# Causal attention inside a two-layer kernel: three single score banks in place of two double ones, and a third bank for the rough maxima

## The reference

```
q = (x @ Wq).reshape(B, T, H, Dh)        # B=2, T=1024, H=16, Dh=16; x is layer-normed
k = (x @ Wk).reshape(B, T, H, Dh)
v = (x @ Wv).reshape(B, T, H, Dh)
scores = jnp.einsum('bthd,bshd->bhts', q, k)
mask = jnp.tril(jnp.ones((T, T), dtype=scores.dtype))
scores = scores * mask                    # masked scores are 0, not minus infinity
attn = jax.nn.softmax(scores / T ** 0.5, axis=-1)
out = jnp.einsum('bhts,bshd->bthd', attn, v).reshape(B, T, H * Dh)
return out @ Wo
```

## Time and profile before

| what | value |
|---|---|
| median of 3 runs | 2155.03 us |
| the profiled execution's own time | 2154.63 us |
| its span | 2152.9 us |
| PE busy | 1960.6 us (91%) |
| DVE busy | 1253.0 us (58%) |
| ACT busy | 822.5 us (38%) |
| POOL busy | 889.0 us (41%) |
| attention: start of its first instruction on DVE, first slot, last values | about 272, 342 and 693 us |
| a middle group's 24 slots (group 4) | 44.0 us |

### The profile page before, as it was taken

The page is one execution under the profiler, slowest core; times in us unless marked ns, Lnnn a source line. Parts: engine busy times, 40 slices in busy tenths (PEclk is TensorE's granted clock), DMA queues, the critical chain, the costliest instruction groups (busy, mean ns, idle before and its releaser), DMA issues. The chain is left out here.

```text
span 2152.9 us, 29698 instructions
## 1 busy us (share of the span) xinstructions
PE 1960.6 (91%) x8876; PEld 1279.2 (59%) x8876; DVE 1253.0 (58%) x2704; ACT 822.5 (38%) x1549; POOL 889.0 (41%) x708
## 2 busy tenths in 40 slices
PE   5899958999999789986779999999889999999987
PEld 5676635555655757655646555555566656565566
DVE  6322264666775722227667777777656777777526
ACT  2122243555655212223324444444514444444413
POOL 0344410343223044432026655666425555665732
PEclk9999967999999589997679999999999999999999
DMA  9111241111110811124232212222032222221001
GB/s 395 52 62 64 57 130 30 31 44 32 44 30 1 353 59 60 66 68 166 45 81 56 55 46 52 55 58 58 19 70 59 55 59 59 58 52 46 24 0 52
DMA packets 64617, 150.91 MB, mean 70 GB/s; under 512 B 14320, under 2 KB 19648, under 8 KB 62208
## 3 DMA queue, kind: packets, MB, share of 16 engines
q1 hardware_dynamic: 54240, 120.44, 19.6%
q0 software_dynamic: 9120, 24.92, 3.7%
q10 hardware_dynamic: 1152, 4.19, 0.5%
HBM read 68.95 MB, written 18.61 MB: 41 GB/s over the span
## 5 line engine op out<-in xcount | busy, mean ns | idle before, releaser
L1858 POOL TENSOR_TENSOR mla_PS<-mla_PS,mla_PT 128x1024 f32<-128x1024 f32 x192 | 457.5, 2383 | 232.6 <-ACT mla_PT L2142 225.3
L2142 ACT ACTIVATE mla_PT<-PS 128x512 f32<-128x512 f32 x512 | 297.2, 600 | 390.9 <-PE PS L1962 322.9
L2275 DVE TENSOR_REDUCE mla_MXP<-PS 128x1 f32<-128x512 f32 x512 | 320.9, 679 | 94.9 <-PE PS L1943 94.4
L1971 PE MATMUL PS<-mla_PT,mla_CN 128*64 128x512 f32 x1024 | 249.4, 607 | 2.3 <-ACT mla_PT L2142 2.3
L1283 DVE TENSOR_REDUCE att_MX<-PS 128x1 f32<-128x512 f32 (+3 forms) x304 | 194.2, 660 | 89.7 <-PE PS L994 49.3
L522 DVE COPY moe_HT<-PS 128x256 f32<-128x256 f32 x188 | 70.4, 415 | 299.9 <-PE PS L648 299.9
L2287 DVE RECIPROCAL PS<-PS 128x128 f32<-128x128 f32 x128 | 114.9, 936 | 180.4 <-PE PS L1978 180.4
L1962 PE MATMUL PS<-mla_QH,mla_KH 113*128 113x512 f32 x512 | 216.1, 422 | 0.9 <-ACT mla_PT L2142 0.9
L684 POOL DMA_INDIRECT moe_XS<-rows_in,moe_GI x96 | 93.7, 976 | 266.1 <-PE PS L634 130.8
L1943 PE MATMUL PS<-mla_KH,mla_QH 113*128 113x512 f32 x512 | 184.8, 429 | 20.6 <-DMA mla_KL<-mla_SL 14.0
L1962 PE MATMUL PS<-mla_QL,mla_KH 113*128 113x512 f32 x512 | 202.4, 395 | 0.0
(11 more groups left out here) (295 smaller groups left out, 3175.8 us busy)
## 6 DMA issues: line engine op xcount, KB each, us to landing
W<-in_W_dram SPq DMA_DIRECT2D x16, 2048.0 KB, 28.1
mla_QH<-mla_SH SPq DMA_DIRECT2D x64, 128.0 KB, 2.4
mla_KH<-mla_SH SPq DMA_DIRECT2D x64, 128.0 KB, 2.4
mla_QL<-mla_SL SPq DMA_DIRECT2D x64, 128.0 KB, 2.4
mla_KL<-mla_SL SPq DMA_DIRECT2D x64, 128.0 KB, 2.4
mla_KH<-mla_SH SPq DMA_DIRECT2D x64, 96.0 KB, 2.3
mla_KL<-mla_SL SPq DMA_DIRECT2D x64, 96.0 KB, 2.4
sums_Y<-rows_out SPq DMA_DIRECT2D x9, 512.0 KB, 6.3
```

The source lines that it names most:

```text
L1858: pool.tensor_tensor(PS[:, :], PT[:, slot(0), :] if k == 1 else PS[:, :], PT[:, slot(k), :], ALU.add).then_inc(s_ps.handle, 1)
L1971: ins = pe.matmul(bank(6)[h * DKVL:(h + 1) * DKVL, :], CN[:, b, k, 0:DKVL], PT[:, slot(k), h * HB:(h + 1) * HB], start=(k == 0), stop=(k = ...
L2142: act.activation(PT[:, slot(k), h * HB:(h + 1) * HB], bank(st_bank(s, h))[:, :], ACT.Exp, scale=MLA_SCALE).then_inc(s_p.handle, 1)
L2275: dve.tensor_reduce(MXP[:, n // NPC, c, h, t:t + 1], bank(piece_bank(n))[:, :], AX_X, ALU.max).then_inc(s_mx.handle, 1)
```

## The change

Scores take three single banks in rotation. The unit is now one head of a slot: unit u = 2s + head has bank 2 + u % 3 and waits for the exponential of unit u-3. Each unit's matmul signals ACT by itself, and ACT runs one exponential a unit, 384 of them in place of 192, half as wide. The bank that this frees, 5, becomes a third one for the rough pieces: 0, 1 and 5 in rotation, counted over all groups, and piece n waits for the maximum of piece n-3. The counts of all who wait for scores or exponentials (SP, POOL, PE's values) are converted to the new units.

```diff
-        st_banks = lambda n: banks(2 + 2 * (n % 2), 2).rearrange("p (h s) -> p h s", h=2)
+        st_bank = lambda s, hh: bank(2 + (2 * s + hh) % 3)
+        piece_bank = lambda H, n: bank((0, 1, 5)[(NPC * H + n) % 3])
         MISC = bank(7)
+        NU = 2 * NSL
+        assert NU % 3 == 0
...
-                        if NPC * H + n >= 2:
-                            pe.wait_ge(s_mx.handle, s_mx.at(NPC * H + n - 1))
+                        if NPC * H + n >= 3:
+                            pe.wait_ge(s_mx.handle, s_mx.at(NPC * H + n - 2))
                         i = 4 * q + t
-                        out = bank(n % 2)[:, 0:len(hs) * w].rearrange("p (h k) -> p h k", k=w)
+                        out = piece_bank(H, n)[:, 0:len(hs) * w].rearrange("p (h k) -> p h k", k=w)
...
-                    if NSL * G + s >= 2:
-                        pe.wait_ge(s_p.handle, s_p.at(NSL * G + s - 1))
                     c0 = columns(q, j)
                     for hh in range(2):
-                        ins = pe.matmul(st_banks(s)[:, hh, c0:HB], KT[:, G % 2, pair, j * P:(j + 1) * P], QT[:, G % 2, 2 * pair + hh, q * HB + c0:(q + 1) * HB],
-                                        start=True, stop=True)
-                    ins.then_inc(s_st.handle, 1)
+                        unit = NU * G + 2 * s + hh
+                        if unit >= 3:
+                            pe.wait_ge(s_p.handle, s_p.at(unit - 2))
+                        pe.matmul(st_bank(s, hh)[:, c0:HB], KT[:, G % 2, pair, j * P:(j + 1) * P], QT[:, G % 2, 2 * pair + hh, q * HB + c0:(q + 1) * HB],
+                                  start=True, stop=True).then_inc(s_st.handle, 1)
...
-                    act.wait_ge(s_st.handle, s_st.at(NSL * G + s + 1))
                     if NKEY * G + kk >= 2:
                         act.wait_ge(s_v.handle, s_v.at(NKEY * G + kk - 1))
                     pair = s % 2
-                    act.activation(PT[:, kk % 2, 2 * pair:2 * pair + 2, c0:HB], st_banks(s)[:, :, c0:HB], ACT.Exp, scale=SEQ ** -0.5).then_inc(s_p.handle, 1)
+                    for hh in range(2):
+                        act.wait_ge(s_st.handle, s_st.at(NU * G + 2 * s + hh + 1))
+                        act.activation(PT[:, kk % 2, 2 * pair + hh, c0:HB], st_bank(s, hh)[:, c0:HB], ACT.Exp, scale=SEQ ** -0.5).then_inc(s_p.handle, 1)
```

More of the change, by code:

```diff
@@ L831, in _ @@
                         if G >= 2:
-                            sp.wait_ge(s_st.handle, s_st.at(NSL * (G - 2) + 2 * TB if half else NSL * (G - 1)))
+                            sp.wait_ge(s_st.handle, s_st.at(NU * (G - 2) + 4 * TB if half else NU * (G - 1)))
                         tok = slice(half * HB, (half + 1) * HB)
@@ L866, in cut_later_keys @@
                     part = PT[:, s // 2 % 2, 2 * (s % 2):2 * (s % 2) + 2, c0:c0 + P]
-                    pool.wait_ge(s_p.handle, s_p.at(NSL * G + s + 1))
+                    pool.wait_ge(s_p.handle, s_p.at(NU * G + 2 * s + 2))
                     pool.affine_select(part, part, [[0, 2], [1, P]], ALU.is_ge, 0.0, base=0, channel_multiplier=-1).then_inc(s_cut.handle, 1)
@@ L887, in clear_max_rows @@
                     q = HALF[r]
-                    pool.wait_ge(s_st.handle, s_st.at(NSL * (H - 1) if r else NSL * (H - 2) + 2 * TB))
+                    pool.wait_ge(s_st.handle, s_st.at(NU * (H - 1) if r else NU * (H - 2) + 4 * TB))
                     if r:
@@ L1022, in values_of @@
                     else:
-                        pe.wait_ge(s_p.handle, s_p.at(NSL * G + 2 * kk + 2))
+                        pe.wait_ge(s_p.handle, s_p.at(NU * G + 4 * kk + 4))
                     if G == 0 and kk == 0:
@@ L1281, in maxima @@
                         dve.wait_ge(s_sh.handle, s_sh.at(NPC * H + n + 1))
-                        part = bank(n % 2)[:, 0:len(hs) * w].rearrange("p (h k) -> p h k", k=w)
+                        part = piece_bank(H, n)[:, 0:len(hs) * w].rearrange("p (h k) -> p h k", k=w)
                         ins = dve.tensor_reduce(MX[:, q, c, hs[0]:hs[-1] + 1, t], part, AX_X, ALU.max)
```

## The result

The kernel after the change takes 2135.29 us (median of 4 runs, 2133.46 to 2138.21) against 2155.46 us before (4 runs, 2154.64 to 2156.91): a ratio of 0.991, 95% interval 0.9896 to 0.9924. The forecast was 2136.5 us. The profiled execution took 2133.46 us with a span of 2131.7.

A forecast was written before the change was run, and what follows sets the result against it. PE sets the pace, losing time waiting on maxima; ahead of slot 0 PE and DVE take turns. Terms -5.5, -17.9 and +5.0 give -18.4 us, forecast 2136.5 us; range 2132 to 2142 (60%), wider 2129 to 2149.

The forecast's parts named there:

- term 2: Rough pieces' waits in the slots: the third bank starts each piece one maximum sooner, -17.9 us (bounds -20 and -10).
- term 1: 27 rough pieces ahead of slot 0: with three banks DVE should never wait, -5.5 us.
- rival E: Ahead of slot 0 the clock rises as PE gets denser, and losses of term 4 are nil: 2130.3 us, 15%.
- term 4: Scores on three banks: late second heads in short slots cost 3.2 us, plus 0.8 in slots 6 of groups 5 to 7.
- the rest 0.2: Piece waits in slots other than 0, 10, 14, 16, 18 and 21: 0.2 us a group, to be gained.
- rough-load waits under half of 53.0 and only in slot 10: Sign in the next profile's wait list: rough loads behind maxima wait under half of 53.0 us, only in slot 10.
- Term 3: One exponential a unit on ACT: nothing by itself in middle groups, 1.0 us charged in group 7.
- slots 1, 3 and 7, under 0.3 us each: Sign in the next profile: score loads wait for exponentials in these slots, under 0.3 us each.
- rival A: Odd slots' second heads wait for exponentials because ACT is behind in short even slots: 29 us lost, about 2160.6, 7%.
- B: Ahead of slot 0 nothing is gained, because the transfers' queue sets their end at 364.45 us: 2142 us, 10%.
- C: Added waits on 192 score loads cost 0.1 us each even when satisfied: +19 us, so no change, 2155 us, 4%.
- D: The clock falls within the slots, in seven groups as in group 2: 26 us eat the gain, 2162 us, 4%.

## Why the prediction was right, step by step

The forecast was a change of -18.4 us; measured medians give -20.2, -16.7 and -16.7. The terms as measured come to -5.8 and about -1 ahead of slot 0, -14.6 for the piece waits, and for scores and exponentials +3.7 against the trace of before or +5.5 by the experiments (5.10 for the bank, 0.36 for the split): -17.7 or -15.9 us. The two differ mainly in groups 0 and 2, whose stretches at 0.50 are of different length from trace to trace. So the total was right while single terms were not: term 2 promised 3.3 us too much and group 7's price was too low, while the clock, left out of term 1, gave about 1 us. That it came out so near is in part luck.

**Term 1, the pieces ahead of slot 0 (-5.5).** Right in mechanism, and near in its own part, -5.8. What I had put into rival E, the clock, came on top, but it is smaller than these two traces say. From last maximum to slot 0 it takes 8.09 us in two traces of the changed kernel and 9.03 in the third, with its short return to the lower level; with two banks 8.71, 8.90, 9.02 and, before, 10.25. That is about 1 us where the clock stays up, nothing in the third trace, and not 2.2. It isn't the 3 us of rival E either: that took the stretch for 6.8 us at the upper level, and it is 8.09. The run with unread matmuls speaks for the denser PE as the cause of the rise. I had named the rise, and kept it out of the sum. The other half of E, no losses in term 4, is false. "DVE without idle time" held but for the one pause of 0.55 us, and slot 0 came at 336.26 us (forecast near 337).

**Term 2, piece waits in the slots (-17.9).** The step that was mis-sized, at 2.75 us a group. Against the kernel with two piece banks put back it is 2.24 to 2.30 in groups 1, 3, 4 and 5 and 14.6 us in all. Slots 14, 16 and 18 gained what I had priced (0.37, 0.34, 0.49 for 0.40, 0.33, 0.47) and slot 21 more (0.46 for 0.38). Slot 10 gained 0.59 and not 0.74, slot 0 0.19 and not 0.26, which slot 1 lost again, and "the rest 0.2" nothing to speak of. The "same in groups 1 to 6" failed in group 6, with 1.87: its slots 14 to 16 gained 0.29 us together, where group 4's gained 0.71. Group 2's cover by the cut was sized right: 1.23 us, about 1.0 less than its neighbours, for 0.8. The sign that I had named for this term, rough-load waits under half of 53.0 and only in slot 10, failed: 35.7 us remain, because a load that waits under value matmuls costs nothing and is listed all the same. The distances between starts were the right measure and the list was not.

**Term 3 (1.0, in group 7).** Free in the middle groups as forecast, 0.36 in group 7. Slot 23 is 0.34 us longer by it, nearly as much as in the changed kernel, so that slot's loss isn't the banks'.

**Term 4, three score banks (3.2 + 0.8).** Slots 1 and 3 lost 0.21 and 0.28 us for 0.2 and 0.2, slot 1 only once slot 0 was shorter, as the prediction's own reading of it has it. With two piece banks, groups 1, 3, 4, 5 and 6 lost 0.27, 0.53, 0.26, 0.60 and 0.62 against before, 2.3 us for 2.75. But the cause that I gave for slot 3, the copy ahead of the exponential, is wrong: moving it changed nothing, and one piece more in each of slots 0 and 2 took 0.34 us of the 0.49 of slots 1 and 3 out. The sign "slots 1, 3 and 7, under 0.3 us each" held in slots 1 and 3 (loads waited 0.23 to 0.31 us) and not in slot 7, where three waited 0.48 to 0.72; most of the other new waits are the odd slots of group 7.

Group 7 is where the sum was short: 3.3 us instead of at most 1.7 (1.0 of term 3, 0.45 and 0.25 of term 4). The weight-load track of the changed kernel there:

```profile
659.79 0.19 PEld L1018 LDWEIGHTS PS<-att_QT,att_KT 128*128 128x128 f32 x1 [0.40 <-ACT att_PT L1181]
...
662.08 0.19 PEld L1018 LDWEIGHTS PS<-att_QT,att_KT 128*128 128x128 f32 x1 [0.50 <-ACT att_PT L1181]
```

and ACT in between:

```profile
661.65 1.24 ACT L1181 ACTIVATE att_PT<-PS 128x256 f32<-128x256 f32 x4 [0.48 <-PE PS L1018]
```

Each waits for the other. The second head of an odd slot waits for the exponential that frees its bank, and ACT for the matmul behind that load. Without rough pieces in between, seven odd slots (7, 9, 11, 13, 15, 19 and 21) lost 0.1 to 0.7 us. That is rival A's mechanism, confined to the one group without cover. The four-bank kernels (28.05 and 28.31 us for 31.02) show that all but the 0.36 us of the split is the bank count.

**Rivals.** A holds in the main only in group 7. B is false: the transfer wait moved along whole (7.3 us). C is false by the extra wait. D did not come: group 1 ran at a granted clock of 1.00 and group 2 at 0.96, and from 477.6 us to the last exponential it stayed at 1.00. The Trainium skill (TensorE: Matmul & The Clock Gate, A second HAM failure mode: psum-queue depth-cycling) tells of a kernel whose clock swings because PE, cycling through PSUM banks, often idles briefly. What the prediction drew from that, that fewer score banks could bring D, was not borne out here: the 39 score waits, three times as many as before, went with no lower clock.

## What to carry to other kernels

Price a bank by its loop, from matmul start through its reader to the next load (here 1.1 to 1.2 us), and compare it with the shortest stretch of other work beside it: PE has spare banks where rough work fills the slots, and none in a last group where it ends, so a rotation may change where the work does. Read PE's loss from distances between starts and not from the list of waits. Where a two-engine loop runs at the lower clock, ask what its density will be after the edit: here a rise added about 1 us to a saving of 5.8, in two of three traces.

## What the hardware showed that I had not expected

Adding 27 matmuls that nobody reads to a stretch at 1.2 GHz made it about 4 us shorter (27.23 us for 30.94 to 32.48, one run); the granted clock rose to 1.00 some 5 us behind the first maximum. Whether the clock falls again some 10 us after its rise varied between executions of the same kernel (24.47 or 25.41 us to slot 0), and why isn't settled. Nor is it settled why the stretch behind the attention, in which the change has no code, differed by up to 6 us between traces (1457.2 to 1463.0 us).
